# Four graph networks on one core: the first spreading pass takes the relation score from the edge record, groups its fp32 gather products, and loads its source one-hots

## The reference, cut to what matters

```python
h = _layernorm(x, ln_gamma[l], ln_beta[l])
s_h = _node_scores(h, W_h[l], att_h[l])              # (nodes, 2 heads)
s_t = _node_scores(h, W_t[l], att_t[l])
s_r = _node_scores(relation_embed, W_r[l], att_r[l]) # (500 relations, 2 heads)
scores = jax.nn.leaky_relu(s_h[src] + s_t[dst] + s_r[edge_type])
w = _segment_softmax(scores, src, n)
A = 0.85 * w
Z = h broadcast to both heads
for _ in range(3):
    Z = jax.ops.segment_sum(A[:, :, None] * Z[dst], src, num_segments=n) + 0.15 * h[:, None, :]
ent = Z.reshape(n, 128) @ W_o[l] + x
```

## Time and profile before

| what | value |
|---|---|
| median of 3 runs | 13115.35 us (13096.33 to 13125.02) |
| the profiled execution, its own time | 13153.08 us |
| its span, first to last instruction | 13151.2 us |
| TensorE busy (matmul) | 84% of the span |
| TensorE busy (weight load) | 75% |
| VectorE busy | 83% |
| ScalarE busy | 40% |
| GpSimd busy | 18% |
| the two `first_spread` stages | from 7786 to 8683 us and from 10851 to some 11740 us |

### The profile page before, as it was taken

How to read it: one execution, slowest core, us unless ns; L and a number is a source line. 1 busy time by engine, 2 the same in 40 slices (tenths; PEclk the granted TensorE clock), 3 DMA queues, 4 the chain that set the end, 5 groups by cost and what they waited for, 6 DMA issues and landing times. The chain is left out here.

```text
span 13151.2 us, 454466 instructions
## 1 busy us (share of the span) xinstructions
PE 11052.8 (84%) x106619; PEld 9852.5 (75%) x106812; DVE 10871.7 (83%) x40228; ACT 5259.7 (40%) x19197; POOL 2368.9 (18%) x7569
## 2 busy tenths in 40 slices
PE   3455399999999999966665789999997779999999
PEld 2444278899899899955553359999997339999999
DVE  6444489788688588876666999999998999999999
ACT  1000022233233222245452348865453328875454
POOL 2777400000000000011110002222221002222222
PEclk9999999899899799989887999999998999999999
DMA  1111167544344011123333554432222554432222
GB/s 56 45 45 48 55 197 236 171 130 129 95 129 122 21 41 41 41 66 88 73 79 86 145 130 115 114 83 73 70 73 63 145 136 115 115 97 73 70 73 65
DMA packets 1206852, 1233.14 MB, mean 94 GB/s; under 512 B 218352, under 2 KB 1042801, under 8 KB 1206107
## 3 DMA queue, kind: packets, MB, share of 16 engines
q1 hardware_dynamic: 1180954, 1228.47, 34.8%
q0 software_dynamic: 25792, 3.35, 0.2%
HBM read 1115.06 MB, written 116.16 MB: 94 GB/s over the span
## 5 line engine op out<-in xcount | busy, mean ns | idle before, releaser
L1034 DVE TENSOR_SCALAR hot<-iota_row,place 128x128 f32<-128x128 f16 (+1 forms) x9000 | 1860.8, 288 | 141.3 <-PE acc L1133 103.0
L1752 ACT ACTIVATE msgs<-G,share 128x64 f32<-128x64 f32 x6000 | 1399.3, 317 | 1341.9 <-PE G L1766 1341.9
L1026 DVE TENSOR_SCALAR hotT<-idx,iota_col 128x512 bf16<-128x512 f16 x4500 | 1363.4, 371 | 520.9 <-PE G L1179 480.9
L1766 PE MATMUL G<-u_b,hotT 128*128 x12000 | 1591.5, 276 | 50.5 <-DVE hotT L1700 50.5
L1776 PE MATMUL S<-msgs,hot 128*128 128x128 f32 x12000 | 1586.4, 275 | 0.0
L1198 ACT CAST msgs<-G 128x384 bf16<-128x384 f32 x2250 | 1024.2, 482 | 1352.8 <-PE G L1179 1348.1
L1766 PEld LDWEIGHTS G<-u_b,hotT 128*128 128x128 f32 x12000 | 1466.6, 193 | 51.2 <-issue 51.2
L1776 PEld LDWEIGHTS S<-msgs,hot 128*128 128x128 f32 x12000 | 1462.4, 192 | 0.0
L1151 ACT ACTIVATE msgs<-sums 128x128 f32<-128x128 f32 x2250 | 703.0, 312 | 1702.0 <-DVE sums L1143 1105.8
L1121 PE MATMUL G<-table_m,hotT 128*128 x9000 | 1303.3, 248 | 93.7 <-issue 70.6
L1015 POOL COPY place<-e 128x4 f32 (+1 forms) x2250 | 452.2, 201 | 4883.2 <-DVE hot L1034 4258.0
(11 more groups left out here) (321 smaller groups left out, 19718.2 us busy)
## 6 DMA issues: line engine op xcount, KB each, us to landing
idx<-pos_rows SPq DMA_DIRECT2D x6375, 128.0 KB, 3.1
hotT<-hots_d SPq DMA_DIRECT2D x750, 256.0 KB
hots_d<-hotT SPq DMA_DIRECT2D x375, 256.0 KB, 3.5
key_b<-key_rows SPq DMA_DIRECT2D x62, 416.0 KB
ty_b<-type_rows SPq DMA_DIRECT2D x62, 416.0 KB
rows<-rel_rows SPq DMA_DIRECT2D x1500, 6.0 KB
ew_now<-ew_rows_d SPq DMA_DIRECT2D x1125, 3.0 KB
sorted_d<-recs,place POOLq DMA_INDIRECT x806
```

The lines of the kernel that those rows point to most:

```text
L1026: op = eng.tensor_scalar(hotT[:, c % deep, n], idx[:, c, r], p.col[:, first:first + 1], None, ALU.is_equal)
L1034: op = eng.tensor_scalar(hot[:, c % 2, q], p.row16[:], place[:, c % 2, q:q + 1], None, ALU.is_equal)
L1752: op = eng.activation(msgs[:, c % 2, 2 + j // HEADS, j % HEADS * D:(j % HEADS + 1) * D], G[c % 2][1][:, j * D:(j + 1) * D], ACT.Copy, scal ...
L1766: mm = eng.matmul(G[c % 2][b][:, k * W:(k + 1) * W], hotT[:, c % 2, q * P:(q + 1) * P], table[:, ds(dst_at(at, q, 24 * W), W)], start=True ...
```

## The change

Relation score: `rows`, `s.picks` and the third product of each chunk are gone. POOL copies two words of each edge's record into columns 12 and 13 of `terms` (`relate`, one for each quarter, issued a step ahead, between its two other copies), and `add_up` waits for it and sums four terms of each column where there were three; `terms` is set to zero once ahead of the pass. The records of empty places get -2^100 as relation score at the program's start. Gather: the four fp32 products of a quarter are issued in a row, the first with the start flag for the whole bank, and after them the four bf16 products. Source one-hots: SP loads `near` for each quarter, 128 rows of 512 columns, from `s.hots_d` (four buffers, where the load of `rows` stood and behind the same wait), and the load of source positions and the DVE instruction that made `near` are gone.

```diff
@@ -1421,16 +1421,15 @@
     Q = QUARTERS
     V = W + HEADS
     with ctx:
-        idx = p.sb("idx", [P, 4, 2, 4 * P], FP16, ctx)
+        idx = p.sb("idx", [P, 4, 4 * P], FP16, ctx)
         hotT = p.sb("hotT", [P, 2, 4 * P], FP32, ctx)
-        near = p.sb("hotS", [P, 2, 4 * P], BF16, ctx)
-        rows = p.sb("rows", [P, 4, 4, P], BF16, ctx)
+        near = p.sb("hotS", [P, 4, 4 * P], BF16, ctx)
         hot = p.sb("hot", [P, 2, 4, P], FP32, ctx)
         place = p.sb("place", [P, 2, 4], FP32, ctx)
-        terms = p.sb("terms", [P, 2, 4, 6 * HEADS], FP32, ctx)
+        terms = p.sb("terms", [P, 2, 4, 8 * HEADS], FP32, ctx)
         total = p.sb("total", [P, 2, 4, 2 * HEADS], FP32, ctx)
-        totals = p.sem("totals")
-        to0 = totals.at
+        totals, related = p.sem("totals"), p.sem("related")
+        to0, rl0 = totals.at, related.at
         totals.at += Q
         bent = p.sb("bent", [P, 2, 4, HEADS], FP32, ctx)
         less = p.sb("less", [P, 2, 4, HEADS], FP32, ctx)
@@ -1447,43 +1446,49 @@
         tu0, h0, pl0, sh0, sc0, f0, te0, b0, le0, k0 = (x.at for x in (
             turned, hots, placed, shared, scattered, folded, termed, bends, lessed, kept))
         g0, m0 = gathered.at, made.at
-        on_vector(p, [lambda e: e.memset(rows[:], 0.0)])
+        on_vector(p, [lambda e: e.memset(terms[:], 0.0)])
 
         with p.block() as block:
             @block.sync
             def _(eng):
                 def step(t, c):
                     reach(eng, turned, tu0, t - 3)
-                    for r in range(2):
-                        eng.dma_start(idx[:, c, r], s.pos_rows[1 - r][ds(t * (4 * P), 4 * P)].partition_broadcast(P)
-                                      ).then_inc(idx_in[c].h, 16)
+                    eng.dma_start(idx[:, c], s.pos_rows[1][ds(t * (4 * P), 4 * P)].partition_broadcast(P)
+                                  ).then_inc(idx_in[c].h, 16)
                     reach(eng, gathered, g0, t - 3)
-                    at = 3 * HEADS * l
-                    eng.dma_start(rows[0:3 * HEADS, c],
-                                  s.rel_rows[ds(t * 4, 4), at:at + 3 * HEADS, :].rearrange("k r e -> r k e")
+                    eng.dma_start(near[:, c], s.hots_d[ds(t, 1), :, 0:4 * P].rearrange("o p e -> p (o e)")
                                   ).then_inc(idx_in[c].h, 16)
                 quarters(eng, step)
                 for c in range(4):
-                    idx_in[c].at += 48 * ((Q - c + 3) // 4)
+                    idx_in[c].at += 32 * ((Q - c + 3) // 4)
 
             @block.gpsimd
             def _(eng):
+                def relate(t, c):
+                    reach(eng, totals, to0, t - 1)
+                    at = REL + HEADS * l
+                    eng.tensor_copy(terms[:, c % 2, :, 6 * HEADS:7 * HEADS], s.e[:, ds(t * 4, 4), at:at + HEADS]
+                                    ).then_inc(related.h, 1)
+
                 def step(t, c):
                     reach(eng, hots, h0, t - 1)
                     eng.tensor_copy(place[:, c % 2].unsqueeze(2), s.e[:, ds(t * 4, 4), 0:1]).then_inc(placed.h, 1)
+                    if not (isinstance(t, int) and t == Q - 1):
+                        relate(t + 1, (c + 1) % 4)
                     reach(eng, shared, sh0, t + 1)
                     eng.tensor_copy(s.score[:, ds(t * 4, 4), :], msgs[:, c, :, W:V]).then_inc(kept.h, 1)
+                relate(0, 0)
                 quarters(eng, step)
                 placed.at += Q
+                related.at += Q
                 kept.at += Q
 
             @block.vector
             def _(eng):
                 def gather_hots(t, c):
-                    arrived(eng, idx_in[c], i0[c], t, c, 48)
+                    arrived(eng, idx_in[c], i0[c], t, c, 32)
                     reach(eng, gathered, g0, t - 1)
-                    eng.tensor_scalar(hotT[:, c % 2], idx[:, c, 0], p.col[:, 0:1], None, ALU.is_equal)
-                    eng.tensor_scalar(near[:, c % 2], idx[:, c, 1], p.col[:, 0:1], None, ALU.is_equal).then_inc(turned.h, 1)
+                    eng.tensor_scalar(hotT[:, c % 2], idx[:, c], p.col[:, 0:1], None, ALU.is_equal).then_inc(turned.h, 1)
 
                 def scatter_hots(t, c):
                     reach(eng, scattered, sc0, t - 1)
@@ -1494,6 +1499,7 @@
 
                 def add_up(t, c):
                     reach(eng, termed, te0, t + 1)
+                    reach(eng, related, rl0, t + 1)
                     eng.tensor_reduce(total[:, c % 2], terms[:, c % 2].rearrange("p k (i r) -> p k r i", r=2 * HEADS), AX.X, ALU.add
                                       ).then_inc(totals.h, 1)
 
@@ -1578,7 +1584,7 @@
                 def pick(t, c):
                     reach(eng, gathered, g0, t + 1)
                     reach(eng, lessed, le0, t - 1)
-                    eng.copy(terms[:, c % 2], G[c][:].rearrange("p (k f) -> p k f", f=W)[:, :, D:D + 6 * HEADS]
+                    eng.copy(terms[:, c % 2, :, 0:6 * HEADS], G[c][:].rearrange("p (k f) -> p k f", f=W)[:, :, D:D + 6 * HEADS]
                              ).then_inc(termed.h, 1)
 
                 def product(t, c):
@@ -1609,13 +1615,15 @@
             def _(eng):
                 def gather(t, c, at):
                     reach(eng, turned, tu0, t + 1)
+                    to = [G[c][:, q * W:(q + 1) * W] for q in range(4)]
                     for q in range(4):
-                        to = G[c][:, q * W:(q + 1) * W]
-                        eng.matmul(to, hotT[:, c % 2, q * P:(q + 1) * P],
-                                   table[:, ds(dst_at(at, q, 24 * W), W)], start=True, stop=False)
-                        eng.matmul(to[:, D:2 * D], near[:, c % 2, q * P:(q + 1) * P],
-                                   s.own[:, ds(src_at(at, 24 * SMALL), D)], start=False, stop=False)
-                        mm = eng.matmul(to[:, D:2 * D], rows[:, c, q], s.picks[:], start=False, stop=True)
+                        eng.matmul(to[q], hotT[:, c % 2, q * P:(q + 1) * P],
+                                   table[:, ds(dst_at(at, q, 24 * W), W)], start=(q == 0), stop=True,
+                                   skip_group_check=True)
+                    for q in range(4):
+                        mm = eng.matmul(to[q][:, D:2 * D], near[:, c, q * P:(q + 1) * P],
+                                        s.own[:, ds(src_at(at, 24 * SMALL), D)], start=False, stop=True,
+                                        skip_group_check=True)
                     mm.then_inc(gathered.h, 1)
 
                 def scatter(t, c, now):
@@ -1897,7 +1905,6 @@
         s.q_most = p.sb("q_most", [P, BLK * SMALL], FP32, ctx)
         s.far = p.sb("far", [P, P], BF16, ctx)
         s.pick = p.sb("pick", [P, HEADS, P], BF16, ctx)
-        s.picks = p.sb("picks", [P, D], BF16, ctx)
         odd = p.sb("odd", [P, 2], I32, ctx)
         odds = p.sb("odds", [P, 2], FP32, ctx)
         s.rz = p.sb("rz", [P, BLK, HEADS], FP32, ctx)
@@ -1928,8 +1935,7 @@
             lambda e: e.tensor_copy(odds[:, 1:2], odd[:, 1:2]),
             lambda e: e.tensor_scalar(odds[:, 0:1], odds[:, 1:2], -1.0, 1.0, ALU.mult, ALU.add)]
             + [lambda e, r=r: e.tensor_scalar(s.pick[:, r], p.ones[:], odds[:, r:r + 1], None, ALU.mult) for r in range(HEADS)]
-            + [lambda e: e.memset(s.picks[:], 0.0), lambda e: e.tensor_copy(s.picks[:, 0:HEADS], odds[:]),
-               lambda e: e.memset(s.own[:], 0.0)])
+            + [lambda e: e.memset(s.own[:], 0.0)])
         relation_rows(p, s)
         for l in range(LAYERS):
             h = s.cat[:, :, 0:D]
@@ -2033,7 +2039,8 @@
                     eng.memset(s.empty[:], 0.0).then_inc(pool.h, 1)
                     eng.wait_ge(pool.h, pool.at + 2)
                     eng.memset(s.empty[:, :, 0:2], float(NONE)).then_inc(pool.h, 1)
-                    pool.at += 3
+                    eng.memset(s.empty[:, :, REL:2 * REL], -FAR).then_inc(pool.h, 1)
+                    pool.at += 4
             count_buckets(p, s)
             place_buckets(p, s)
             relation_scores(p, s)
```

## The result

The changed kernel takes 12891.64 us (median of 4 runs, 12880.71 to 12898.78) against 13110.38 before (4 runs): ratio 0.9832, 95% interval 0.9815 to 0.9849, 219 us less. Its profiled execution has a span of 12890.3 us.

What follows compares the result with a forecast made beforehand. PE was taken to bound first_spread at 2.34 us a step; PE 1.99, DVE 1.96 and ACT about 1.9 to 2.1 gave 2.01. Saving 0.33 over 750 steps, 248 us, gave 12867 us, range 12830 to 12950.

Steps and rivals of the forecast that it cites:

- PE bounds the kernel before: In the two first_spread stages PE never waits and fills the 2.34 us period; DVE is close at 2.16.
- PE's new step, 1.99: PE's time per first_spread step: 0.89 fp32 products, 4 x 0.03 bf16, 0.08 change of kind, 0.90 scatter, in us.
- 0.08 for a change of kind: Extra PE time in the gather for changing between fp32 and bf16 products, 0.08 us, paid once instead of four times.
- 0.03 for a bf16 product: PE time of one bf16 gather product, 0.03 us; upper end 0.06.
- DVE's new step, 1.96: DVE's time per first_spread step without the source one-hot instruction: 1.96 us, ends 1.91 and 2.08.
- step in which it does not wait: A DVE step read from the old profile, 2.06 us, base of DVE's new step; 0.10 was added for the branch.
- ACT, 1.85 to 2.10: ACT's unchanged work per first_spread step: 2.00 us, ends 1.85 and 2.10, leaving nearly no idle time.
- POOL, 0 to 0.04: What POOL's added copy can cost DVE beside it: 0 to 0.04 us a step; its own time costs nothing.
- SP and the DMA: The 128 KB load of near costs nothing: 3.1 us landing against 3.98 us available, 0.9 to spare.
- Step 2.01: The new first_spread period, from PE 1.99, DVE 1.96, ACT about 1.9 to 2.1, not fully evened out: 2.01 us.
- Rival 1: DVE, ACT or POOL's copy takes over as bound, step 2.05 to 2.16 us; chance 0.23.
- Rivals 2, 3 and 4: Grouping gives nothing, 13002 to 13025 us, 0.08; late near load, 13423, 0.03; unseen chain or lower PE clock, 0.04.

Runs made afterwards that it cites:

- e7: Kernel before with only the source one-hots loaded instead of made on DVE: 13033.96 us, ratio 1.0000.
- e1: Changed kernel with DVE's sum reading three terms of each column instead of four, relation score left out: 12766.47 us, ratio 0.9798.
- e3: Changed kernel with the gather products in the old order, each bf16 product behind its chunk's fp32 product: 12947.82 us, ratio 0.9938.
- e9: Kernel before with source one-hots loaded and gather products grouped, relation rows still loaded and multiplied: 12851.70 us, ratio 0.9863.
- e10: Changed kernel with the source one-hots made on DVE again from loaded positions: 12989.11 us, ratio 0.9966.
- e2: Changed kernel without POOL's relation copy and the wait for it, fourth term zero: 12799.62 us, ratio 0.9824.
- e11: Changed kernel with 256 KB loaded for each quarter from the stored one-hots, only the first half used: 12799.56 us, ratio 0.9819.

## Why the prediction was right, and where its sum was off

The forecast was 12867 us, 248 less than before; measured are 219 less, the profile's stages say 235. By its steps:

- **PE bounds the kernel before:** right. Taking the whole source one-hot from DVE (e7) changed nothing.
- **PE's new step, 1.99:** right, 1.98 in e1. Of its two terms the 0.08 for a change of kind is shown by e3, the 0.03 for a bf16 product by e9 against e1: 2.10 - 1.98 = 0.12 for four. "TensorE: Matmul & The Clock Gate" of the Trainium skill, section Back-to-back issue gap, gives some 81 ns for a pair of load and matmul of 128 columns; at 64 columns a pair took 0.03 here, so its figure does not carry over.
- **DVE's new step, 1.96:** this is the mis-sized term; it measured 2.012 and 2.04. Three pieces of it were off. The removed instruction was right: 0.26 by e10 against the changed kernel (2.271 - 2.010, 2.298 - 2.041). The wait for POOL's copy was put at 0.05 and cost nothing. The fourth term was put at 0.02 and cost 0.05 to 0.06: now the next instruction starts 0.17 us after the reduction (8001.40 to 8001.57), and in the kernel before it was 0.12, in the same view:

```profile
8107.36 0.20 DVE L1497 TENSOR_REDUCE total<-terms 128x16 f32<-128x48 f32 x1
8107.48 0.28 DVE L1516 TENSOR_TENSOR acc<-S,acc 128x130 f32 x1
```

  And the "step in which it does not wait", 2.06 us, was the quickest of the four in a turn, the one with 0.08 between less and hotT. A full turn has 0.08, 0.17, 0.20 and 0.57, a mean of 0.26, where the prediction reckoned with 0.08 and 0.10 for the branch. 1.96 - 0.05 + 0.04 + 0.08 = 2.03, near both stages, and inside the ends of 1.91 and 2.08 that it gave for DVE.
- **ACT, 1.85 to 2.10:** it was at its lower end, 1.84, so its cover never ran out.
- **POOL, 0 to 0.04:** nothing. Its own copies do get longer, the new one:

```profile
L1470 POOL COPY terms<-e x750: 189/236/327, 7753.5 to 11466.5; 128x8 f32 x184, 128x8 f32<-128x8 f32 x4
```

  a median of 236 ns where its quickest takes 189; DVE's distances are the same with this copy and without it (e2), so it is POOL that gives way. The full lock of "SBUF — State Buffer" in the Trainium skill, section SBUF: two separate sides, which it gives for a DVE instruction in a 2-port mode or with two inputs in SBUF, would have put 0.20 us on DVE. No run here shows that for these instructions.
- **SP and the DMA:** nothing, as forecast, with more to spare than the 0.9 us: the load landed in 2.1 us, not 3.1, and one of twice the size cost nothing either (e11).
- **Step 2.01:** right in the first stage (2.012), 0.03 short in the second (2.041), because DVE, which I had below PE, is above it. That it fits the first stage is in part luck. I had it as PE's 1.99 and 0.02 for buffers that do not quite even out the steps. Where PE is the bound no such loss is seen (1.982 in e1, 2.101 in e9, PE's own sums), and the 2.01 is DVE's own step: a loss that did not occur stood in for a DVE term that was too small. 0.03 x 375 = 12 us, the whole of what the stages' 235 lack to 248. The measured 219 has an interval of 198 to 243 by the ratio's, which holds the 235 and not the 248. Rival 1 named DVE as a bound, but from 2.05 on. Rivals 2, 3 and 4 did not occur.

## What to carry to other kernels

When two engines are within a few per cent of each other, take from both: each part of this change alone gave 0 to 0.6%, the three together 1.75%. Try the parts together before dropping one that gives nothing alone, as the loads did. Average an engine's unhurried step over a whole turn of its hardware loop before comparing it with another engine, for steps that read alike differed by 0.12 us and the branch added 0.4 more. And a matmul busy share of 1.00 doesn't prove that PE is the bound; lighten the other engine and see.

## What was unexpected

The same loop code costs DVE different amounts at its end: 0.57 us from less to hotT in the first stage and 0.49 in the second, 0.46 and 0.68 when POOL's copy and the wait for it are left out, 0.45 and 0.49 in e7 and e9, which differ from the changed kernel in other ways. What sets it is open. That is up to 0.05 us a step, more than POOL's copy, the wait for it and the doubled load together. A loop twice as long halves what it costs a step. And a cheap branch doesn't make a short turn: the second stage has the cheaper branch and the longer period.
